# Gathering the experts' rows by token lists in place of scattering them: a state-space layer and a mixture of experts on one core

## The chip, the core and the metric

The kernel runs on one core of a Trainium2 chip. The metric is device time in microseconds (us) of one execution, the median of three runs. A second number is the span of a profiled execution, from its first instruction to its last.

## What is computed

Two batches of 1024 tokens of width 256 pass a state-space layer and then a mixture of experts, each behind a layer norm with a modulation computed from a small vector. Cut to what matters:

```python
h = _layernorm(x) * (1 + ca) + sa
x = x + ga * mamba(h)            # 512 channels x 16 states: h[t] = dA[t] * h[t-1] + dBu[t]; y = sum_s(h * C)
h = _layernorm(x) * (1 + cb) + sb
x = x + gb * ffn(h)              # 8 experts, top 2 of each token

gate_logits = einsum('bsd,de->bse', h, gate_kernel)
top_k_weights, top_k_indices = top_k(gate_logits, 2); weights = softmax(top_k_weights)
inter = silu(h @ w0[e]) * (h @ w1[e])
out = sum over the token's two experts of weight * (inter @ wo[e])
```

## The kernel before

The program is written out by hand for the five engines, each with its own instruction stream; semaphores order them. "Rows" of a tile are its 128 partitions. There are four stages.

**Stage A, projections.** A loop over the 2 batches. PE multiplies the normed tokens with the weights for x, dt, B and C (`project`, L449 to 453), always 128 channels x 1024 tokens into two PSUM banks. DVE copies each C product (`copy_C`, L978 to 983) into one of two slots of `C_st`, and SP stores the slot to `C_scratch` in DRAM twice (`C_to_dram`, L314 to 317), under two semaphores that `copy_C` waits for before it writes the slot again. B goes out in three bf16 parts (L329, 330). After the loop PE computes z (L512 to 516), 8 products into two pairs of banks, and ACT takes each through silu into `szT`, which lies over `C_st`; so ACT first waits until all copies of C have landed (L782 to 784). Stage A ends with a barrier of PE, DVE, ACT and POOL: each drains and raises `a_over`, and all wait for 4 (L517, L790, L1024, L1296; SP at L342).

**Stage B, scans.** 8 groups of 128 channels x 16 states, 128 steps in all. For a step PE spreads B over the partitions (`front`), DVE multiplies it with `du` (`drive`, L1033; for 4 of 16 states ACT copies it out and POOL multiplies, `share`, L1333), ACT computes the decay (L800), DVE scans 1024 tokens (L1045), POOL multiplies with C (`weigh`, L1310), and PE sums over states (`back`, L553). The C of a step comes from DRAM into one of four slots of `crep` (L356): 16 stored rows (8 heads, each there twice), each read for 8 partitions; a slot is asked for again when the product from it is done. Every second step SP also sends 261 KB of zeros to the rows' scratch (`zeros`, L337 to 339; `expert_in_scratch`, 17408 rows). A second barrier, `b_over`, ends the stage.

**Stage C, output projection and routing.** PE projects 16 tiles of 128 tokens (`outward_y`), DVE adds them to x and norms them, PE turns each tile (`turn_h2`, L593) and computes the gate's logits (L602), DVE picks two experts of each token (`pick`) and finds the place of each pair of token and expert in its expert's list (`place_of`, L1145 to 1158) from counts that PE makes (`ranks`, L605 to 617). This goes in quarters of 4 tiles, one quarter behind the other in DVE's fixed order (L1163 to 1197). POOL writes the 2048 tokens' rows, 261 numbers each, to the places, with one indirect DMA for each tile and each of the two choices: 32 (`send`, L1356). Small tables (L1199 to 1222) then give each of 39 slots of 128 rows its expert and its first row. A third barrier, `c_over`, ends the stage. SP then loads `wo` and waits until all 32 writes have landed (`sent`, L382) before it loads the first slot (L388).

**Stage D, experts.** For each of the 39 slots: SP loads 128 rows (L388) into one of two slots of `xg`, two slots ahead; PE turns them (L639), multiplies with w0 and w1 (L651), turns the product (L659), multiplies with wo (L667); ACT and DVE do the rest between; POOL adds the slot's results into the output with an indirect DMA (L1379), one after the other. In iteration i of the loop PE's order is: turn slot i+2, turn the product of i, hidden product of i+1, output product of i. DVE also takes each row's position, batch, expert and weights out of columns 256 to 260 (L1240 to 1245).

## Time and profile before

| | |
|---|---|
| median of 3 runs | 943.36 us (943.11 to 946.33) |
| profiled execution | 951.12 us, its span 949.3 us |
| granted TensorE clock, mean | 0.914 |
| busy share of the span | PE 79%, DVE 67%, POOL 53%, PEld 39%, ACT 34% |
| chain of waits, by engine | PE 43%, DVE 22%, POOL 10%, issue 10%, DMA 7%, ACT 6% |
| moved by DMA | 137.05 MB, mean 144 GB/s |

All times in this document are us on the profiled execution's own scale, where the first instruction starts at 0. Stage A runs to about 166, stage B from there to 603, stage C to 705, stage D to the end. The busy shares mix these four. The granted clock tells which share of 2.4 GHz TensorE got in a stretch: 1.00 is 2.4 GHz and 0.50 is 1.2 GHz.

### The profile page before, as it was taken

To read this page: it belongs to the slowest core of one execution; us is meant where nothing else is said; L and a number is where in the kernel's file an instruction comes from. 1 tells how busy PE (TensorE), PEld (TensorE's weight loads), DVE (VectorE), ACT (ScalarE), POOL (GpSimd) and SP (SyncE) were. 2 spreads that over 40 slices of the span, in tenths; PEclk is the share of its full clock that TensorE was granted. 3 is DMA by queue.
4 is the path that set the end of the run, shared out by engine and by line. 5 is a ranking of instruction groups with operands and counts; after the bars stand their busy time and mean duration, and the time that the engine had idled before them with its cause. 6 is when DMAs were issued, how large, how long until landed. Compare 5 with 4: busy or idle time off the path is not lost.

```text
span 949.3 us, 10338 instructions
## 1 busy us (share of the span) xinstructions
PE 749.2 (79%) x2240; PEld 368.4 (39%) x2241; DVE 639.7 (67%) x878; ACT 324.5 (34%) x360; POOL 502.0 (53%) x263
## 2 busy tenths in 40 slices
PE   5888969388878687787878787875329999999995
PEld 2433324132322232222323232564215666666663
DVE  4355662599999999899999999555504444444442
ACT  1564663445444444445444444001011111111110
POOL 1000000399999999999999999414622222222222
PEclk9898988599999998989999899986559999999998
DMA  9354540687877777777777688561361222222220
GB/s 260 96 136 146 131 142 0 174 219 200 220 201 213 185 221 192 200 182 217 209 191 213 185 219 221 183 241 68 113 221 35 42 44 44 44 43 43 43 38 0
DMA packets 75004, 137.05 MB, mean 144 GB/s; under 512 B 11426, under 2 KB 47586, under 8 KB 74852
## 3 DMA queue, kind: packets, MB, share of 16 engines
q1 hardware_dynamic: 64620, 127.97, 48.5%
q0 software_dynamic: 7152, 8.48, 5.3%
q10 hardware_dynamic: 3208, 0.34, 0.3%
q8 instruction: 8, 0.13, 0.1%
q14 instruction: 16, 0.13, 0.0%
HBM read 93.82 MB, written 39.66 MB: 141 GB/s over the span
## 4 chain that ended last, share of the span: by engine, by line
PE 43%; DVE 22%; POOL 10%; issue 10%; DMA 7%; ACT 6%; SPq 2%; ACTq 1%; POOLq 1%; DVEq 0%
DVE pool L1045 16%; PE PS L651 14%; PE PS L667 7%; PE PS L452 7%; PE PS L553 6%; ACT PS L800 4%; POOL pool L1310 4%; DMA C_scratch<-Y 4%; PE PS L584 3%; POOL spread L1333 3%; POOL expert_in_scratch L1360 2%; PE PS L659 2%; DVE pool L1033 2%; PE PS L535 1%; PE PS L639 1%
## 5 line engine op out<-in xcount | busy, mean ns | idle before, releaser
L1310 POOL TENSOR_TENSOR pool<-pool,hT 128x1024 f32<-128x1024 f32 x128 | 298.6, 2358 | 21.3 <-PE PS L553 17.4
L553 PE MATMUL PS<-pool,ident 128*128 128x512 f32 x512 | 261.1, 634 | 45.5 <-POOL pool L1310 45.3
L1045 DVE TENSOR_TENSOR_SCAN pool<-PS,pool 128x1024 f32<-128x1024 f32 x96 | 215.7, 2274 | 0.0
L800 ACT ACTIVATE PS<-pool,negA 128x1024 f32 (+1 forms) x128 | 143.1, 1118 | 195.9 <-DVE pool L1045 195.8
L1379 POOL DMA_INDIRECT out<-uT,ptab x39 | 60.6, 1554 | 184.3 <-DVE uT L1256 177.7
L553 PEld LDWEIGHTS PS<-pool,ident 128*128 128x128 f32 x512 | 96.0, 197 | 154.4 <-POOL pool L1310 74.8
L1033 DVE TENSOR_TENSOR pool<-PS,pool 128x1024 f32<-128x1024 f32 x96 | 117.6, 1225 | 40.9 <-PE PS L535 31.6
L651 PE MATMUL PS<-pool,uT 128*128 x312 | 142.6, 600 | 0.8 <-ACT uT L864 0.4
L535 PE MATMUL PS<-pool 96*128 96x512 bf16 x256 | 81.8, 403 | 54.7 <-DVE pool L1033 44.2
L1302 POOL TENSOR_TENSOR pool<-pool,uT 128x1024 f32<-128x1024 f32 (+1 forms) x8 | 18.9, 2359 | 143.0 <-ACTq L790 143.0
L1230 DVE TENSOR_TENSOR uT<-uT,PS 128x512 f32<-128x512 f32 x39 | 26.9, 689 | 92.8 <-PE PS L651 90.0
L1333 POOL TENSOR_TENSOR spread<-spread,pool 128x1024 f32<-128x1024 f32 x32 | 75.6, 2363 | 13.9 <-ACT spread L806 13.9
L651 PEld LDWEIGHTS PS<-pool,uT 128*128 128x128 f32 x312 | 57.0, 193 | 58.6 <-issue 58.6
L1045 DVE TENSOR_TENSOR_SCAN pool<-PS,spread 128x1024 f32<-128x1024 f32 x32 | 73.1, 2283 | 9.4 <-POOL spread L1333 9.4
L535 PEld LDWEIGHTS PS<-pool 96*128 96x128 bf16 x256 | 21.1, 101 | 149.0 <-DVE pool L1033 99.8
L667 PE MATMUL PS<-Y,uT 128*128 x312 | 73.8, 379 | 0.9 <-DVE uT L1235 0.9
L452 PE MATMUL PS<-hT,pool 128*128 x112 | 59.7, 686 | 12.2 <-DVE Y L983 12.2
L667 PEld LDWEIGHTS PS<-Y,uT 128*128 128x128 f32 x312 | 59.2, 190 | 25.3 <-issue 19.3
L864 ACT ACTIVATE uT<-PS 128x256 f32<-128x256 f32 x39 | 15.0, 385 | 144.1 <-PE PS L639 144.1
L870 ACT ACTIVATE uT<-PS 128x512 f32<-128x512 f32 x39 | 23.3, 598 | 74.6 <-PE PS L651 74.6
L1360 POOL DMA_INDIRECT expert_in_scratch<-pool,posu x32 | 31.7, 990 | 28.0 <-DVEq L1158 18.9
L806 ACT ACTIVATE spread<-PS 128x1024 f32<-128x1024 f32 x32 | 32.8, 1024 | 35.0 <-PE PS L535 35.0
(163 smaller groups left out, 699.9 us busy)
## 6 DMA issues: line engine op xcount, KB each, us to landing
hT<-C_scratch SPq DMA_DIRECT2D x128, 512.0 KB, 5.7
expert_in_scratch<-zrow SPq DMA_DIRECT2D x68, 261.0 KB, 5.8
C_scratch<-Y SPq DMA_DIRECT2D x16, 512.0 KB
pool<-in_w SPq DMA_DIRECT2D x16, 512.0 KB, 10.0
uT<-expert_in_scratch SPq DMA_DIRECT2D x39, 130.5 KB, 2.1
Y<-Y SPq DMA_DIRECT2D x32, 128.0 KB, 2.4
Y<-in_wo SPq DMA_DIRECT2D x8, 512.0 KB, 10.5
x_tok<-in_x SPq DMA_DIRECT2D x4, 512.0 KB, 8.9
```

What stands on the lines that cost most here:

```text
L452: m = pe.matmul(PS[:, bank + half, :], w(k), rhs(k, half), start=k == 0, stop=k == k_chunks - 1)
L535: m = pe.matmul(PS[:, 4 + half, :], sel[0:PARTS * 32, k, :], stk[0:PARTS * 32, r, HF * half:HF * half + HF], start=True, stop=True)
L553: m = pe.matmul(PS[:, 6 + half, :], ident[:, :], prod[:, k % PR, HF * half:HF * half + HF], start=False, stop=k == DS - 1)
L651: m = pe.matmul(PS[:, bank, :], xgT[:, r, k, :], w[:, bass.ds(e, 1), k, :].rearrange("p e n -> p (e n)"), start=k == 0, stop=k == KD - 1)
L667: m = pe.matmul(PS[:, 6 + r, 0:DM], intT[:, r, k, :], wo_sb[:, bass.ds(e, 1), k, :].rearrange("p e n -> p (e n)"), start=k == 0, stop=k == ...
L800: act.activation(pair(2 * (k % 2)).unsqueeze(1), delta[:, bass.ds(g2 * 2 + r, 1), :], ACT.Exp, scale=decay[:, bass.ds(g2 * (2 * DS) + n, 1 ...
L1033: dve.tensor_tensor(dbu[:, owned_to(k) % 2, :], pair(4), du[:, r, :], ALU.mult).then_inc(dbu_done, 1)
L1045: dve.tensor_tensor_scan(hst[:, k % HR, :], pair(2 * (k % 2)), driven, 0.0, ALU.mult, ALU.add).then_inc(scan_done, 1)
L1310: gp.tensor_tensor(prod[:, k % PR, :], hst[:, k % HR, :], crep[:, k % RC, :], ALU.mult).then_inc(prod_done, 1)
L1333: gp.tensor_tensor(spread[:, :], spread[:, :], du[:, r, :], ALU.mult).then_inc(shared_done, 1)
L1360: gp.indirect_dma_start(out=xs_dram, out_offset=bass.IndirectOffsetOnAxis(ap=posu[:, i, t:t + 1], axis=0), in_=h2row[:, t, :], in_offset=N ...
L1379: gp.indirect_dma_start(out=out, out_offset=bass.IndirectOffsetOnAxis(ap=ptab[:, slot:slot + 1], axis=0), in_=yo[:, slot % 2, :], in_offse ...
```

## The change

**C and B in DRAM.** C is stored once, by one DMA whose source and target are both 128 rows of 1024; the stored array has 8 rows for a step, and the load of a step reads each of them for 16 partitions. B goes out in four DMAs of 32 partitions x 3 parts.

**Barriers.** `a_over` and `b_over` are gone; each engine waits for the semaphores of the data that it uses. SP loads the first B parts after the first product of z, and the first C after the last. The decay rates (`negA`) are computed early in stage A. At the end of stage B PE runs the projection of tiles 0 to 2 between its last sums (before those of states 14 and 15).

**Rows by gather.** The zeros and the 32 writes are gone. Tokens' rows (260 numbers) go to DRAM in the tokens' own order, by 4 plain DMAs from SP. For each pair of token and expert its place p is split into p/128 and p mod 128; DVE makes a one-hot of each (16 operations for a quarter, one of each pair times the token's distance from the end), and PE multiplies the two, 8 products for a quarter, all added up in one PSUM bank: a table of tokens by place. One more product picks, for each slot, its row of that table. POOL then gathers each slot's 128 rows with an indirect DMA (`rows_of`, L1371), two slots ahead of the adds in its own order; `wo` is loaded in stage C.

```diff
-        C_dram = nc.dram_tensor("C_scratch", (2 * NB * DIN, L), F32, kind="Internal").ap()
-
-        C_twice = C_dram.rearrange("(h d s) n -> h d s n", d=2, s=DS)
-        C_rows = C_dram.rearrange("(h s) n -> h s n", s=DS)
+        C_dram = nc.dram_tensor("C_scratch", (NB * DIN, L), F32, kind="Internal").ap()
...
-                    for d, landed in enumerate((C_out[c % 2], C_again[c % 2])):
-                        sp.dma_start(C_twice[bass.ds(b * (DIN // DS) + c * HC, HC), d], C_st[:, c % 2, :]).then_inc(landed, 16)
+                    sp.dma_start(C_dram[bass.ds(b * DIN + c * P, P), :], C_st[:, c % 2, :]).then_inc(C_out[c % 2], 16)
...
-                for part in range(PARTS):
-                    sp.dma_start(B_dram[bass.ds(b * CH, CH), part], B_parts[:, part, :]).then_inc(B_out, 16)
+                for c in range(CH):
+                    sp.dma_start(B_dram[bass.ds(b * CH + c, 1)].rearrange("g a i n -> i (g a) n"),
+                                 B_parts[32 * c:32 * c + 32, :, :]).then_inc(B_out, 16)
...
-            def zeros(i):
-                sp.dma_start(xs_dram[bass.ds(i * (ZS * P), ZS * P), :].rearrange("(n p) c -> p n c", p=P),
-                             zrow[:, :].rearrange("p (n c) -> p n c", c=XW)).then_inc(xs_zeroed, 16)
...
-                                     C_rows[bass.ds((g2 * 2 + r) * 2 * HC, 2 * HC), k, :]
-                                     .unsqueeze(1).broadcast_to([2 * HC, DS // 2, L])).then_inc(crep_in[k % RC], 16)
-                        if k % 2 == 0:
-                            zeros((g2 * 2 + r) * 8 + k // 2)
+                                     C_dram.rearrange("(h s) n -> h s n", s=DS)[bass.ds((g2 * 2 + r) * HC, HC), k, :]
+                                     .unsqueeze(1).broadcast_to([HC, DS, L])).then_inc(crep_in[k % RC], 16)
...
+            sp.wait_ge(z_mm, 1)
             B_of(0, 0)
+            sp.wait_ge(z_mm, NB * CH)
...
-            sp.wait_ge(sent, 16 * 2 * NT)
-
-            def row_of(slot):
-                return sp.value_load(rtab[0:1, bass.ds(slot, 1)], min_val=0, max_val=XR - P)
-
-            def rows_in(first, r):
-                sp.dma_start(xg[:, r, :], xs_dram[bass.ds(first, P), :]).then_inc(xg_in[r], 16)
...
+            def h2_to_dram(q):
+                tiles = slice(TQ * q, TQ * q + TQ)
+                sp.wait_ge(weighted, q + 1)
+                sp.dma_start(h2_dram.rearrange("(t p) c -> p t c", p=P)[:, tiles, :], h2row[:, tiles, :]).then_inc(h2_out, 16)
...
-            pe.drain().then_inc(a_over, 1)
-
-
-            pe.wait_ge(sel_done, 1)
-            pe.wait_ge(a_over, 4)
+            pe.wait_ge(sel_done, HB)
+            pe.wait_ge(dt_free, 1 + NB * CH)
+            pe.wait_ge(C_copied, 1 + NB * CH)
...
+                        if last and r == 1 and k == DS - 2:
+                            outward_y(0)
+                            outward_y(1)
+                        elif last and r == 1 and k == DS - 1:
+                            outward_y(2)
...
+            def tokens_by_place(q):
+                pe.wait_ge(placed, q + 1)
+                for i in range(2):
+                    for j in range(TQ):
+                        m = pe.matmul(PS[:, 3, 0:P], by_place[i][:, j, :], by_row[:, i, j, :],
+                                      start=q == 0 and i == 0 and j == 0, stop=q == NQ - 1 and i == 1 and j == TQ - 1)
+                m.then_inc(place_mm, 1)
...
+            pe.wait_ge(turned_back, 2)
+            pe.matmul(PS[:, 6 + NQ % 2, 0:NS], token_by, slot_at, start=True, stop=True).then_inc(token_mm, 1)
...
-                step(dve.tensor_copy(posu[:, :, tiles], posf[:, q]))
+                step(dve.tensor_copy(pos_i, posf[:, q]))
+                settled()
+                step(dve.tensor_scalar(places[:, 0], pos_i, 7, None, ALU.arith_shift_right))
+                step(dve.tensor_scalar(places[:, 1], pos_i, P - 1, None, ALU.bitwise_and))
+                settled()
+                step(dve.tensor_copy(place_f, places))
+                settled()
+                if q:
+                    dve.wait_ge(place_mm, q)
+                else:
+                    dve.wait_ge(noted, 2)
+                for i in range(2):
+                    for j in range(TQ):
+                        step(dve.tensor_scalar(by_place[i][:, j, :], iota128, place_f[:, 0, i, j:j + 1],
+                                               from_end[:, TQ * q + j:TQ * q + j + 1], ALU.is_equal, ALU.mult))
+                        step(dve.tensor_scalar(by_row[:, i, j, :], iota128, place_f[:, 1, i, j:j + 1], None, ALU.is_equal))
...
+            dve.tensor_scalar(slot_at, slot_at, since[:, :], None, ALU.is_equal).then_inc(turned_back, 1)
+            dve.wait_ge(place_mm, NQ)
+            dve.tensor_copy(token_by, PS[:, 3, 0:P]).then_inc(turned_back, 1)
+            dve.wait_ge(token_mm, 1)
+            step(dve.tensor_scalar(ptab[:, :], PS[:, 6 + NQ % 2, 0:NS], -1.0, float(T), ALU.mult, ALU.add))
+            settled()
+            step(dve.tensor_scalar(gtab[:, :], ptab[:, :], float(T - 1), None, ALU.min))
...
-            def send(q):
-                gp.wait_ge(placed, q + 1)
-                for t in range(TQ * q, TQ * q + TQ):
-                    for i in range(2):
-                        gp.indirect_dma_start(out=xs_dram, out_offset=bass.IndirectOffsetOnAxis(ap=posu[:, i, t:t + 1], axis=0),
-                                              in_=h2row[:, t, :], in_offset=None).then_inc(sent, 16)
...
+            def rows_of(slot):
+                gp.indirect_dma_start(out=xg[:, slot % 2, :], out_offset=None, in_=h2_dram,
+                                      in_offset=bass.IndirectOffsetOnAxis(ap=gtab[:, slot:slot + 1], axis=0)).then_inc(xg_in[slot % 2], 16)
+
+            def refill(slot):
+                gp.wait_ge(xT_mm, slot - 1)
+                gp.wait_ge(meta_done, 3 * (slot - 1))
+                rows_of(slot)
+
...
+            gp.wait_ge(c_over, 3)
+            gp.wait_ge(h2_out, 16 * NQ)
+            rows_of(0)
+            rows_of(1)
+            gp.wait_ge(x2_out, 16 * NQ)
+            gp.sem_inc(yo_free, 2)
+            refill(2)
+            for slot in range(NS):
+                if slot + 3 < NS:
+                    refill(slot + 3)
+                leave(slot)
```

What moves, in the order of the engines' rows. On SP, the stores of stage A, for one batch; the name left of the arrow is the scratch in DRAM, and the sizes are the target's. Before:

```order
L330 DMA B_parts_scratch<-pool 4x32x1024
L330 ISA
L330 DMA B_parts_scratch<-pool 4x32x1024
L317 ISA [waits C_copied]
L317 DMA C_scratch<-Y 8x16x1024
L317 ISA
L317 DMA C_scratch<-Y 8x16x1024
```

and now:

```order
L331 DMA B_parts_scratch<-pool 32x3x1024
L331 ISA
L331 DMA B_parts_scratch<-pool 32x3x1024
L318 ISA [waits C_copied]
L318 DMA C_scratch<-Y 128x1024
```

One store for each C product, and outer sizes of 32 and 128 in place of 4 and 8.

On DVE, `place_of` in stage C, one quarter (`hT` holds the routing's small tables). Before:

```order
L1148 TENSOR_TENSOR hT<-PS,hT 128x32 [waits rank_mm]
L1152 TENSOR_TENSOR hT<-hT 128x64 [waits route_step]
L1154 TENSOR_REDUCE hT<-hT 128x8 [waits route_step]
L1156 CAST posu<-hT 128x2x4 [waits route_step]
L1096 SCALAR_TENSOR_TENSOR hT<-x_tok,mv,grow 128x256 [waits route_step,aggr2_done,h2_rows]
```

and now (six pairs like the two shown follow before L1090):

```order
L1150 TENSOR_REDUCE hT<-hT 128x8 [waits route_step]
L1152 CAST hT<-hT 128x8 [waits route_step]
L1154 TENSOR_SCALAR hT<-hT 128x8 [waits route_step]
L1155 TENSOR_SCALAR hT<-hT 128x8
L1157 CAST hT<-hT 128x16 [waits route_step]
L1165 TENSOR_SCALAR hT<-hT,from_end 128x128 [waits noted,route_step]
L1167 TENSOR_SCALAR spread<-hT 128x128
L1165 TENSOR_SCALAR hT<-hT,from_end 128x128
L1167 TENSOR_SCALAR spread<-hT 128x128
```

The 16 one-hots stand between the places and the norm of the next quarter.

On POOL, from the routing into stage D. Before:

```order
L1360 DMA expert_in_scratch<-pool,posu 17408x261 [waits placed]
L1360 DMA expert_in_scratch<-pool,posu 17408x261 x7
L1360 DMA expert_in_scratch<-pool,posu 17408x261 [waits placed]
L1360 DMA expert_in_scratch<-pool,posu 17408x261 x7
L1379 DMA out<-uT,ptab 2048x256 [waits x2_out,yo_done]
L1379 DMA out<-uT,ptab 2048x256 [waits yo_done,added] x38
```

and now:

```order
L1372 DMA uT<-expert_in_scratch,gtab 128x260 [waits h2_out,c_over]
L1372 DMA uT<-expert_in_scratch,gtab 128x260
L1372 DMA uT<-expert_in_scratch,gtab 128x260 [waits x2_out,meta_done,xT_mm]
L1372 DMA uT<-expert_in_scratch,gtab 128x260 [waits meta_done,xT_mm]
L1385 DMA out<-uT,ptab 2048x256 [waits yo_done]
L1372 DMA uT<-expert_in_scratch,gtab 128x260 [waits meta_done,xT_mm]
L1385 DMA out<-uT,ptab 2048x256 [waits yo_done,added]
L1372 DMA uT<-expert_in_scratch,gtab 128x260 [waits meta_done,xT_mm]
```

The gather of slot i+4 stands directly behind the add of slot i; before, the loads were on SP and stood behind no add.

## Rows read from the trace of the kernel before

**Rows 1.** costliest groups of the page: shapes, count, busy us, mean ns, idle before, releaser
```profile
L1310 POOL TENSOR_TENSOR pool<-pool,hT 128x1024 f32<-128x1024 f32 x128 | 298.6, 2358 | 21.3 <-PE PS L553 17.4
```

**Rows 2.** DMA issues of the page: count, KB each, median us from issue to landing
```profile
hT<-C_scratch SPq DMA_DIRECT2D x128, 512.0 KB, 5.7
expert_in_scratch<-zrow SPq DMA_DIRECT2D x68, 261.0 KB, 5.8
...
uT<-expert_in_scratch SPq DMA_DIRECT2D x39, 130.5 KB, 2.1
```

**Rows 3.** stretches: us, busy by engine, PEclk, share of 16 DMA engines, GB/s
```profile
119.00:122.00 3.00, 2.10 (x5) 0.68 (x4) 0.11 (x1) 2.97 (x4) 0.00 (x0) 1.00 0.51 209
250.00:300.00 50.00, 40.76 (x100) 15.10 (x100) 48.56 (x28) 22.92 (x22) 47.27 (x21) 0.97 0.77 206
650.00:683.00 33.00, 14.06 (x95) 10.60 (x95) 21.11 (x113) 3.47 (x11) 22.31 (x23) 0.50 0.23 82
```

**Rows 4.** the chain of waits: start us, us, what
```profile
56.63 16.20 DMA C_scratch<-Y
...
130.97 8.73 DMA C_scratch<-Y
```

**Rows 5.** DVE in time, stage A: start, us, instruction, idle before and releaser
```profile
72.86 1.22 DVE L983 COPY Y<-PS 128x1024 f32<-128x1024 f32 x1 [6.76 <-DMA C_scratch<-Y]
```

**Rows 6.** PE in time, stage A and its end
```profile
74.14 6.54 PE L452 MATMUL PS<-hT,pool 128*128 x8 [4.50 <-DVE Y L983]
82.24 7.13 PE L452 MATMUL PS<-hT,pool 128*128 x16 [1.56 <-DVE Y L983]
...
123.17 5.40 PE L452 MATMUL PS<-hT,pool 128*128 x8 [2.08 <-DVE Y L983]
...
142.49 23.67 PE L452 MATMUL PS<-hT,wz_sb 128*128 x48 [7.05 <-ACT Y L788]
```

**Rows 7.** PE in time, the first product of stage B
```profile
175.23 1.03 PE L535 MATMUL PS<-pool 96*128 96x512 bf16 x2 [9.08 <-DMA pool<-B_parts_scratch]
```

**Rows 8.** POOL in time, the first shared step of stage B
```profile
182.35 2.35 POOL L1333 TENSOR_TENSOR spread<-spread,pool 128x1024 f32<-128x1024 f32 x1 [12.40 <-ACT spread L806]
```

**Rows 9.** PE in time, end of stage B
```profile
601.26 1.98 PE L553 MATMUL PS<-pool,ident 128*128 128x512 f32 x4 [0.32 <-POOL pool L1310]
604.49 14.08 PE L584 MATMUL PS<-wout,uT 128*128 128x256 f32 x64 [1.24 <-ACTq L835]
```

**Rows 10.** DVE in time, eight 128x256 operations with two column operands
```profile
16.72 2.67 DVE L908 TENSOR_SCALAR Y<-x_tok,mv,rstd 128x256 f32<-128x256 f32 x8 [1.76 <-POOL rstd L1294]
```

**Rows 11.** PE in time, the routing, and its first work on experts
```profile
652.57 0.69 PE L593 MATMUL PS<-ident,pool 128*128 128x128 f32 x2 [4.85 <-DVE pool L1102]
653.74 1.02 PE L602 MATMUL PS<-gate_sb,hT 128*128 128x8 f32 x4 [0.47 <-ACT hT L844]
...
704.92 0.69 PE L639 MATMUL PS<-ident,uT 128*128 128x128 f32 x2 [29.48 <-DMA uT<-expert_in_scratch]
```

**Rows 12.** DVE in time, after the last table of the routing
```profile
683.07 0.43 DVE L1259 TENSOR_TENSOR grow<-grow 128x256 f32<-128x256 f32 x1
```

**Rows 13.** line 1360, scattered writes: duration ns min/median/max, and landing
```profile
L1360 POOL DMA_INDIRECT expert_in_scratch<-pool,posu x32: 957/961/1303, 651.3 to 696.0; - x32
...
DMA to landing us min/median/max: 2.4/2.8/7.1
```

**Rows 14.** line 1379, adds into the output: the same
```profile
L1379 POOL DMA_INDIRECT out<-uT,ptab x39: 1550/1551/1618, 721.8 to 940.3; - x39
...
DMA to landing us min/median/max: 2.7/3.9/4.5
```

**Rows 15.** PE in time, the first product of two successive slots
```profile
807.41 0.38 PE L639 MATMUL PS<-ident,uT 128*128 128x128 f32 x2
...
813.23 0.38 PE L639 MATMUL PS<-ident,uT 128*128 128x128 f32 x2
```

**Rows 16.** POOL in time, the same stretch
```profile
814.95 1.55 POOL L1379 DMA_INDIRECT out<-uT,ptab  x1 [4.27 <-DVE uT L1256]
```

More of the change, by code:

```diff
@@ L374, in _, with x2_to_out @@
                     sp.dma_start(dst[:, e], src[e].rearrange("(k p) n -> p k n", p=P)).then_inc(w01_in, 16)
-            for q in range(NQ):
+            sp.wait_ge(gated, CH * NB)
+            for e in range(NE):
+                sp.dma_start(wo_sb[:, e], wo[e].rearrange("(k p) n -> p k n", p=P)).then_inc(wo_in, 16)
+            def x2_to_out(q):
                 tiles = slice(TQ * q, TQ * q + TQ)
@@ L555, in back, with outward_y @@
                 m.then_inc(ysum_done, 1)
+            def outward_y(t):
+                b, at = t // NTB, t % NTB * P
+                if t == 0:
+                    pe.wait_ge(folded, 2)
+                    pe.wait_ge(gated, CH)
+                if t in (0, 2):
+                    pe.wait_ge(scan_done, 2 + NG * DS - (t == 0))
+                if t == NTB:
+                    pe.wait_ge(gated, CH * NB)
+                if t >= 3:
+                    pe.wait_ge(x2_step, t - 2)
+                for k in range(CH):
+                    m = pe.matmul(PS[:, t % 3, 0:DM], uT[:, b * CH + k, at:at + P], (wout0, wout_sb)[b][:, k, :],
+                                  start=k == 0, stop=k == CH - 1)
+                m.then_inc(o_mm, 1)
             def blocks_of(g2, last):
@@ L623, in _ @@
                     ranks(stage - 3)
+                    tokens_by_place(stage - 3)
                 for i in range(TQ):
@@ L719, in _, with decay_rates @@
             act.wait_ge(mod_step, 2)
+            def decay_rates():
+                act.wait_ge(acol_in, 16)
+                for n in range(NB):
+                    act.activation(negA[:, n, :], acol[:, :, :].rearrange("p c s -> p (c s)"), ACT.Exp).then_inc(col_done, 1)
             for b in range(NB):
+                if b:
+                    decay_rates()
                 for j in range(2):
@@ L1183, in _ @@
                         gathered(t)
+                if stage == 0:
+                    gate_y(CH + 3)
+                    route_tables()
                 if 0 <= stage - 3 < NQ - 2:
@@ L1207, in _ @@
             step(dve.tensor_tensor_scan(off, onef, cnt, 0.0, ALU.mult, ALU.add))
-            step(dve.tensor_scalar(fall, cnt, float(-P), float(T), ALU.mult, ALU.add))
+            step(dve.tensor_scalar(fall, cnt, float(-NT), None, ALU.add))
             settled()
@@ L1381, in _ @@
                                       compute_op=ALU.add).then_inc(added, 16)
+            for q in range(NQ):
+                rstd_of(q)
+            gp.wait_ge(c_over, 3)
[9 more added lines that the diff above has]
+                leave(slot)
             gp.wait_ge(added, 16 * NS)
```

205 lines of the change are left out of this document (81 added, 124 removed).

## The prediction

> **What bounds the kernel now.** I read the page's busy shares and slices, then the chain of waits, then each stage in time on the engines that wait there, then stretches and DMA rows. PE's 79% is a mean over stages with different limits. In stage A the chain runs through the C stores: one DMA of 16.20 and one of 8.73 us stand on it [rows 4], and DVE waits 6.76 us for a slot [rows 5]. Between A and B, PE runs z for 23.67 us [rows 6] and then waits 9.08 for B [rows 7]. In stage B a step takes (601.26 - 182.35) / 128 = 3.27 us [rows 8, 9]. DVE and POOL share this bound: of 50 us DVE is busy 48.56 and POOL 47.27, PE 40.76 [rows 3]; POOL's product alone is 298.6 us, 2.36 a step [rows 1]. The 16 DMA engines are busy 0.77 of that stretch [rows 3]. In stage C, DVE and PE alternate at a granted clock of 0.50 [rows 3], and behind the last table (683.07) [rows 12] PE waits until 704.92 for the written rows, 29.48 us of idle time [rows 11]. In stage D a slot takes 813.23 - 807.41 = 5.82 us [rows 15]; POOL's add waits 4.27 for its data in it [rows 16], so POOL has room.
>
> **The change part by part.** The sum is made against the profiled execution (951.12), 7.8 us above the median of the runs (943.36); I add it to the median.
>
> 1. *C stores, -15.* For the first batch's C copy DVE gets its slot 6.76 us late, at 72.86 [rows 5]; PE waits for that copy 4.50, and its next 8 matmuls take 6.54, where 16 take 7.13 at the full clock just behind, so 3.57 for 8 [rows 6]: 4.5 + 3.0 = 7.5 us. In the second batch the same place costs 2.08, and 5.40 - 3.57 = 1.83 [rows 6]: 3.9. Together 11.4, if a single store lands within the slot's turn. The stores move 209 GB/s at a share of 0.51 of the engines [rows 3], and half as many bytes go out. The last store holds z's ACT back, and through the PSUM banks PE, 7.05 us [rows 6]; 8.73 us of two DMAs [rows 4] become one of 4.4 (half) to 5.7 (the landing of 512 KB in stage B [rows 2]), so 3 to 4 more. Sum -15, bounds -16 and -11 (last store gives nothing).
> 2. *Barrier and B loads, -9.* z ends at 142.49 + 23.67 = 166.16 [rows 6], B is used at 175.23 [rows 7]. Loads requested behind z's first product are there long before. What comes behind, 182.35 - 175.23 = 7.1 us to the first shared product [rows 7, 8], stays. C is requested behind z's last product and is first needed at the end of those 7.1 us; a load takes 5.7 [rows 2]. If it is late by the rest, -7; if PE's work on B slips in between z's products, -10. I take -9.
> 3. *End of the scans, -2.* Eight tiles of the projection run behind the last sums, 604.49 + 14.08 = 618.57 [rows 9]. A tile is 1.76 us; three of them (5.3) go into waits for POOL's last products, of 2.36 each less 1.98 of sums [rows 1, 9], and most of what they save is met again by DVE's norms. Bounds -3 and 0.
> 4. *Stage B, 0.* The zeros were off the chain. Their cover isn't needed: each of the 128 steps keeps its instructions, and the C load has four slots, so some three steps (9.8 us) of time. This costs nothing as long as a 512 KB load uses the engines for under 3.27 us; see the first rival.
> 5. *One-hots on DVE, +14.* Eight 128x256 operations with two column operands take 2.67 us, 0.334 each [rows 10]. A 128x128 one is between half of it, 0.167, and all of it. I take 0.18, near half, since in such rows the elements carry the time. 16 x 0.18 + three more small operations at 0.2 = 3.5 us a quarter, four quarters 14. They stand in DVE's order ahead of the next quarter's norm, for which PE waits (4.85 before a turn) [rows 11], so all of it is on the path. Bounds 12.8 and 23.7 (0.334 each).
> 6. *Token products on PE, +7.* 8 products a quarter, two matmuls each (f32), at 0.345 (0.69 / 2) or 0.255 (1.02 / 4) [rows 11]: 5.5 or 4.1 us; taken 4.5, at the low clock as now. For the first quarters PE has room while DVE norms, but DVE's wait on the counts stands behind these products in PE's order: 1.5 us each for two of them, and about 4.2 before the last counts. Bounds 0 (all in PE's idle time) and +10.
> 7. *Tail of the tables, +2.5.* Behind the last one-hots come the last 8 products, a copy, one product and two small operations; 4.5 for the products is in point 6, the rest is 2 to 3.
> 8. *Scattered writes gone, -18.* From the last table to PE's first work on experts 704.92 - 683.07 = 21.85 us [rows 11, 12]. Those writes were issued between 651.3 and 696.0, 0.96 each [rows 13]. In their place: 0.9 for the gather's issue and a handoff, and 2.8 to land (median of the writes [rows 13]): -18.1. With points 5 to 7 routing and its tail come out at +5.4. If POOL's norms or the rows' store (82 GB/s is moved there, share 0.23 [rows 3]) come late, the gather comes later; I count that in the bounds.
> 9. *Expert loop, +13.* Here a wait is added: POOL's gather of slot i+4 stands behind the add of slot i. The add starts 7.54 us behind PE's first work of slot i's iteration (814.95 - 807.41) and takes 1.55 [rows 15, 16]. The gather is then asked for at 9.4, and takes L to land. PE needs it two slots later, so 2T >= 9.4 + L. The plain load took 2.1 [rows 2], a scattered write 0.96 + 2.8 less the overlap, an add 3.9 [rows 13, 14]. With L = 2.9, T = 6.15 against 5.82: 38 x 0.33 = +13. Bounds: L = 2.2 gives 5.82, +1; L = 3.9 gives 6.65, +31. I take 2.9 as a gather reads and doesn't add, as the write does.
>
> The Trainium skill bears on this ("DMA: Bandwidth & Descriptors", Anatomy of one DMA, SWDGE path): a GpSimd DMA takes some 2.0 us plus its bytes at 436 GB/s. By that a gather of 133 KB lands in 2.3, an estimate, T is 5.85 and the loss of point 9 is 1 us. The rows of writes and adds lie above it.
>
> Sum: -15 - 9 - 2 + 0 + 14 + 7 + 2.5 - 18 + 13 = -7.5, rounded with the halves -8: **935 us**. Its own range, bounds combined without taking all at their ends: 918 to 955.
>
> **The rivals.**
>
> *The C loads become the bound of the scans (slower).* The load now reads 8 rows, each for 16 partitions. Stores of C with an outer size of 8 kept only 0.51 of the engines busy [rows 3], as if eight of the sixteen worked, while loads with 16 outer rows reach 0.77. If the outer size sets how many work, the loads get eight. In stage B 206 GB/s at 0.77 of 16 engines is 16.7 GB/s each [rows 3]; eight move 134 GB/s, a load needs 3.92 us, and a step grows from 3.27 to 3.92: 128 x 0.65 = +83, at 1018. But in the C stores an engine moved 209 / (0.51 x 16) = 25.6 GB/s [rows 3]; at that rate eight carry 205, a load needs 2.56 and stays hidden. It decides at 524,288 B / 3.27 us = 160 GB/s for the eight. For it: the same bytes are read by sixteen partitions, and the loads' own rate is the low one. Against: the zeros, which share the engines now, are gone, and eight that don't compete may each be faster. Time 955 to 1018. The Trainium skill has the rule ("DMA: Bandwidth & Descriptors", Why a DMA increments its semaphore by 16 and not by 1): a copy is spread over the largest number of engines, up to 16, that divides the outermost dimension of both sides. By that rule the new load gets eight; the trace agrees for the stores of before, and no row of it shows a load with eight rows.
>
> *Gathers are late and the routing is long.* L = 3.9 (+18 over the forecast), or one-hots at 0.334 (+10): about 953. For it: an add takes 3.9 [rows 14]. Against: an add writes and sums, a gather only reads.
>
> *Gathers on time.* Slots stay at 5.85, 12 less: 924. For it: the plain load's 2.1 [rows 2].
>
> *The stores don't get faster.* If a single C store lands as late as the pair (8.73 [rows 4]), stage A keeps its waits and point 1 is lost: 950, the same as no change.
>
> **How the numbers follow.** Forecast 0.38; C loads as the bound 0.28; late 0.12; on time 0.14; stores no faster 0.08. Within 0.5% (all that a measurement of this kernel can tell from no change) is 938.6 to 948.1. Faster: 0.25 of the forecast and the 0.14 on time, 0.40. Same: 0.09 of the forecast (above 938.6, as its bounds of +14 and +31 reach there), 0.02 of late, 0.02 of the loads' case where it is only just missed, 0.05 of the stores': 0.18. Slower: the rest, 0.42, most of it from the C loads. The likeliest case alone gives 918 to 955. The range goes up to 1000, which leaves out the upper end of the C loads' case and little below 918.
>
> **What would show it.** In stage A, DVE's C copies wait for no DMA and z's matmuls end near 151. The first shared product of stage B starts near 158. Stage B: 3.27 us a step means point 4 holds; a longer one with PE, DVE or POOL released by the DMA of C is the first rival, and the landing of C loads (5.7 now [rows 2]) then rises above three steps. A share of 16 engines near 0.5 with the loads hidden shows eight engines that suffice. In stage C: the one-hots' mean (0.18), the token products (4.5 a quarter), first work on experts some 5 us later behind the projection's start than now. In stage D: a slot of 6.15, PE released by the gather, and the gather's landing of 2.9; 5.82 would show the rival on time. What makes the prediction wrong most is a C load above 3.27 us; next a gather's landing, of which each us is 19.

## The result, and the profile after

The changed kernel takes 972.23 us (median of 4 runs, 969.86 to 981.74), the kernel before 943.57 (943.11 to 946.33): a ratio of 1.0316, 95% interval 1.0245 to 1.0388. It is slower; 935 was forecast. The time lies in the range that was given. The first rival, the C loads, is what happened in part, and the expert loop lost more than was counted.

The two profiled executions differ by 971.0 - 949.3 = 21.7 us of span, 7 less than the medians, since the profiled one of before lay 7.8 above its own median. By place (a mark is the start of a row unless said):

| mark | before | after | moved by |
|---|---|---|---|
| end of z | 166.16 | 140.29 | -25.9 |
| first shared product | 182.35 | 147.35 | -35.0 |
| end of POOL's last product with C | 601.21 | 593.15 | -8.1 |
| first product on experts | 704.92 | 697.33 | -7.6 |
| span | 949.3 | 971.0 | +21.7 |

So stage A and the barrier gave 35.0 us, the scans took back 26.9, the routing 0.5, and the expert loop 29.3.

Stage A in time, PE (start, us, instruction, idle before and releaser). The wait of 4.50 before 8 matmuls of 6.54 and the one of 7.05 inside z [rows 6] are gone, and B is there when z ends [rows 7]:

```profile
66.84 3.60 PE L438 MATMUL PS<-hT,pool 128*128 x8
71.84 7.13 PE L438 MATMUL PS<-hT,pool 128*128 x16 [1.41 <-DVE Y L980]
...
112.29 28.00 PE L438 MATMUL PS<-hT,wz_sb 128*128 x64
140.12 0.60 PE L519 MATMUL PS<-pool 96*128 96x512 bf16 x2
```

The first and the last product of the scans, POOL. The last one waits for the DMA of C:

```profile
147.35 2.34 POOL L1351 TENSOR_TENSOR spread<-spread,pool 128x1024 f32<-128x1024 f32 x1 [28.08 <-ACT spread L810]
...
590.59 2.56 POOL L1328 TENSOR_TENSOR pool<-pool,hT 128x1024 f32<-128x1024 f32 x1 [0.74 <-DMA hT<-C_scratch]
```

The chain of waits in the scans (start, us, what). Before, no DMA stood on it there:

```profile
283.35 14.84 DMA hT<-C_scratch
...
300.81 13.61 DMA hT<-C_scratch
...
317.06 13.60 DMA hT<-C_scratch
```

A load is asked for 13.6 to 14.8 us before it lands, four steps at once in the queue, and then POOL runs one product at a time.

Two stretches of the scans (columns as in [rows 3]):

```profile
230.00:365.00 135.00, 96.59 (x214) 35.08 (x215) 107.59 (x61) 50.56 (x47) 109.21 (x48) 0.91 0.51 135
365.00:440.00 75.00, 57.46 (x142) 21.46 (x141) 70.78 (x41) 35.33 (x33) 72.05 (x32) 0.98 0.49 161
```

The share of the 16 engines is one half in both, 0.77 before [rows 3], as if eight of them worked all the time. By the Trainium skill ("DMA: Bandwidth & Descriptors", Why a DMA increments its semaphore by 16 and not by 1) 8 outer rows give eight engines, and here the trace agrees. What those eight move differs: 135 GB/s (16.5 each) in the first stretch, 161 (20.5 each) in the second. POOL does 48 operations in 135 us (2.81 us for each) and 32 in 75 (2.34). The bound that the prediction gave, 160 GB/s, parts the two.

The 161 is what the scans ask for and not what the eight can do. Short windows show that:

```profile
480.00:490.00 10.00, 8.46 (x22) 2.95 (x20) 9.79 (x7) 5.16 (x6) 9.07 (x5) 1.00 0.51 129
500.00:505.00 5.00, 3.72 (x10) 1.26 (x9) 2.60 (x2) 1.55 (x2) 4.43 (x2) 1.00 0.51 192
355.00:360.00 5.00, 4.50 (x9) 1.39 (x8) 3.29 (x2) 0.98 (x1) 5.00 (x3) 0.67 0.51 203
```

At the same share of 0.51 the same kind of load runs at 129 / (0.51 x 16) = 15.8 GB/s for each engine in the first of them, at 23.5 in the second and at 24.9 in the third. These are the two prices of the first rival, 134 and 205, in one execution.

The routing. One-hots by DVE, one pair after the other, and the token products behind the first quarter:

```profile
639.26 0.35 DVE L1165 TENSOR_SCALAR hT<-hT,from_end 128x128 f32<-128x128 f32 x1
639.52 0.28 DVE L1167 TENSOR_SCALAR spread<-hT 128x128 f32<-128x128 f32 x1
639.72 0.34 DVE L1165 TENSOR_SCALAR hT<-hT,from_end 128x128 f32<-128x128 f32 x1
```

```profile
643.09 2.08 PE L613 MATMUL PS<-spread,hT 128*128 128x128 f32 x8 [7.09 <-DVEq L1169]
644.96 1.92 PE L613 MATMUL PS<-spread,by_place 128*128 128x128 f32 x8
...
697.33 0.69 PE L639 MATMUL PS<-ident,uT 128*128 128x128 f32 x2 [4.04 <-DMA uT<-expert_in_scratch,gtab]
```

A pair takes 639.72 - 639.26 = 0.46 us (the rows overlap), so 16 operations some 3.6; PE waits 4.04 where it waited 29.48 [rows 11].

The expert loop, two slots, PE and then POOL. Every second turn waits for a gather:

```profile
732.77 0.43 PE L639 MATMUL PS<-ident,uT 128*128 128x128 f32 x2 [0.54 <-DMA uT<-expert_in_scratch,gtab]
733.04 0.60 PE L659 MATMUL PS<-ident,uT 128*128 128x128 f32 x4
734.00 3.69 PE L651 MATMUL PS<-pool,uT 128*128 x8 [0.36 <-ACT uT L865]
737.54 1.89 PE L667 MATMUL PS<-Y,uT 128*128 x8
739.26 0.38 PE L639 MATMUL PS<-ident,uT 128*128 128x128 f32 x2
...
745.82 0.43 PE L639 MATMUL PS<-ident,uT 128*128 128x128 f32 x2 [0.51 <-DMA uT<-expert_in_scratch,gtab]
```

```profile
741.03 1.59 POOL L1385 DMA_INDIRECT out<-uT,ptab  x1 [4.31 <-DVE wsel L1260]
742.92 0.99 POOL L1372 DMA_INDIRECT uT<-expert_in_scratch,gtab  x1 [0.30 <-issue]
```

Two slots take 745.82 - 732.77 = 13.05 us, 6.53 each against 5.82 [rows 15]. The add starts 8.26 behind the turn, 1.59 and 0.30 follow, and 2.90 behind the start of the gather PE runs again: 13.05.

DMA issues of the page (KB each, median us to landing):

```profile
C_scratch<-Y SPq DMA_DIRECT2D x8, 512.0 KB, 2.6
...
B_parts_scratch<-pool SPq DMA_DIRECT2D x8, 192.0 KB, 3.0
...
uT<-expert_in_scratch,gtab POOLq DMA_INDIRECT x39, 2.8
```

### The profile page after: what moved, and what is told of

Same layout as the page of the kernel before. It is cut to its first block, busy times and chain, and to the rows that moved or that the text cites. A ratio compares the mean times of both kernels' runs of the same rounds, so it can differ in the third digit from the quotient of the medians.

```text
span 971.0 us, 9913 instructions
## 1 busy us (share of the span) xinstructions
PE 771.7 (79%) x2306; PEld 378.9 (39%) x2307; DVE 660.5 (68%) x918; ACT 322.6 (33%) x359; POOL 511.9 (53%) x270
## 4 chain that ended last, share of the span: by engine, by line
PE 36%; DMA 20%; DVE 15%; POOL 14%; issue 9%; ACT 4%; ACTq 0%; DVEq 0%; POOLq 0%; SPq 0%
DMA hT<-C_scratch 13%; PE PS L651 9%; PE PS L438 8%; DVE pool L1037 8%; POOL pool L1328 8%; PE PS L537 6%; DMA uT<-expert_in_scratch,gtab 6%; PE PS L667 3%; PE PS L553 3%; POOL spread L1351 3%; POOL out L1385 3%; ACT PS L804 2%; PE PS L659 2%; PE PS L519 1%; PE PS L639 1%
## 5 line engine op out<-in xcount | busy, mean ns | idle before, releaser
L537 PE MATMUL PS<-pool,ident 128*128 128x512 f32 x512 | 269.8, 652 | 73.9 <-POOL pool L1328 73.7
L651 PE MATMUL PS<-pool,uT 128*128 x312 | 145.2, 608 | 9.1 <-ACT uT L865 7.9
L1037 DVE TENSOR_TENSOR_SCAN pool<-PS,spread 128x1024 f32<-128x1024 f32 x32 | 73.1, 2286 | 25.6 <-POOL spread L1351 25.4
L1372 POOL DMA_INDIRECT uT<-expert_in_scratch,gtab x39 | 38.8, 994 | 69.0 <-DVEq L1243 55.9
L438 PE MATMUL PS<-hT,pool 128*128 x112 | 51.0, 601 | 5.5 <-DVE Y L980 5.5
L810 ACT ACTIVATE spread<-PS 128x1024 f32<-128x1024 f32 x32 | 32.8, 1024 | 35.6 <-PE PS L519 35.6
```

Of the source, the lines that this page charges most:

```text
L438: m = pe.matmul(PS[:, bank + half, :], w(k), rhs(k, half), start=k == 0, stop=k == k_chunks - 1)
L537: m = pe.matmul(PS[:, 6 + half, :], ident[:, :], prod[:, k % PR, HF * half:HF * half + HF], start=False, stop=k == DS - 1)
L651: m = pe.matmul(PS[:, bank, :], xgT[:, r, k, :], w[:, bass.ds(e, 1), k, :].rearrange("p e n -> p (e n)"), start=k == 0, stop=k == KD - 1)
L1037: dve.tensor_tensor_scan(hst[:, k % HR, :], pair(2 * (k % 2)), driven, 0.0, ALU.mult, ALU.add).then_inc(scan_done, 1)
L1372: gp.indirect_dma_start(out=xg[:, slot % 2, :], out_offset=None, in_=h2_dram, in_offset=bass.IndirectOffsetOnAxis(ap=gtab[:, slot:slot + 1 ...
```

## The experiments

The theory after the result: two losses in two stages, C loads on eight engines and gathers queued behind adds. "Scans" below is the time from the start of the first shared product to the end of POOL's last product with C, in the profiled execution: 418.9 us before, 445.8 after. The kernel before took medians of 946.3 to 948.8 beside these runs; each ratio is against its own.

**Gather ahead of the add.**

```diff
             refill(2)
+            refill(3)
             for slot in range(NS):
-                if slot + 3 < NS:
-                    refill(slot + 3)
+                if slot + 4 < NS:
+                    refill(slot + 4)
                 leave(slot)
```

> The changed kernel with one edit: POOL asks for the gather of slot i+4 ahead of the add of slot i, not behind it. If the expert loop grew because each gather is queued behind an add (it is asked for 8.3 us behind the start of the slot's iteration, of 13.1 for two slots), a slot falls from 6.55 back to 5.8 or 5.9 us, PE no longer waits for the gather, and the kernel gets 25 us faster, some 947 us. Rival: the gather itself is too slow, or adds and gathers slow each other in the DMA engines; then a slot stays above 6.3 and the time within 10 us of 972. Stages A to C must not move.

Measured: 946.8 us, single runs 923.2, 946.6, 947.0 and 954.4. The expert loop falls to 952.6 - 706.8 = 245.8 us (244.4 before), and PE no longer waits for a gather:

```profile
821.71 0.38 PE L639 MATMUL PS<-ident,uT 128*128 128x128 f32 x2
...
827.52 0.38 PE L639 MATMUL PS<-ident,uT 128*128 128x128 f32 x2
...
833.34 0.38 PE L639 MATMUL PS<-ident,uT 128*128 128x128 f32 x2
```

5.82 us a slot: the order on POOL was the whole loss of the loop. A gather still lands in 2.8, so it wasn't the gather's own speed. The median moved by 25.4, but the spread of the runs is new. In the profiled run, the slowest of the four, the scans took 452.3 us, with a long slow stretch:

```profile
360.00:495.00 135.00, 95.88 (x212) 34.31 (x212) 105.97 (x60) 51.02 (x47) 105.46 (x46) 0.90 0.52 131
```

That the run of 923.2 had no such stretch is likely, but it has no trace. The slow stretches don't lie where they lay in the changed kernel (some 240 to 350), though the same rows of C are read at the same place in the order; so which rows are read doesn't decide it alone.

**C copied in DRAM, loads over 16 rows.** The store keeps its 128 rows and goes to a scratch of its own; two DMAs for each product then fill the layout of before, in which a load finds its 16 rows.

```diff
+    for d in range(2):
+        sp.dma_start(C_dram.rearrange("(h d s) n -> s d h n", d=2, s=DS)[:, d, rows],
+                     C_once.rearrange("(h s) n -> s h n", s=DS)[:, rows]).then_inc(C_twice, 16)
...
-    C_dram.rearrange("(h s) n -> h s n", s=DS)[bass.ds((g2 * 2 + r) * HC, HC), k, :]
-    .unsqueeze(1).broadcast_to([HC, DS, L])
+    C_dram.rearrange("(h s) n -> h s n", s=DS)[bass.ds((g2 * 2 + r) * 2 * HC, 2 * HC), k, :]
+    .unsqueeze(1).broadcast_to([2 * HC, DS // 2, L])
```

> The changed kernel with C stored once from the SBUF as it is, then copied twice in DRAM (outer size 16 on both sides), so that a load again reads 16 rows, each for 8 partitions. If the scans are slower because a load with an outer size of 8 runs on 8 of the 16 engines, the landing falls, POOL no longer waits for C, and a step falls from 3.44 on average to 3.27 us: 128 steps give 21 us, some 951 us. Stage A stays as in the changed kernel, since nothing on PE's path waits for the copies. Rival: the loads aren't the cause, but the removed barrier or the other order at the start of the scans; then stage B stays at 440 us.

Measured: 949.9 us over ten runs (ratio 1.0027, 1.0000 to 1.0054, without two of them at 959), 22 less than the changed kernel; scans 419.2 us. In the same stretch as above:

```profile
230.00:365.00 135.00, 105.35 (x253) 38.94 (x252) 126.60 (x72) 60.69 (x57) 129.81 (x57) 0.95 0.61 162
```

57 operations on POOL where there were 48. Each engine moves no more than in the slow stretch (162 / 9.8 = 16.6 GB/s), but sixteen can serve. The rate of an engine didn't have to change; their number did. One thing isn't parted here or in any other run: a load over sixteen engines always reads 16 stored rows and a load over eight reads 8. No run reads 8 rows with sixteen engines.

**Both edits.**

> Both edits. The two losses lie in stages that follow one another, so they add: 972 less 21 less 25 gives 926 us, faster than the kernel before by 1.8%. If the gain is under 40 us, one of the two hid behind the other.

Measured: 924.6 us, ratio 0.9756 (0.9715 to 0.9797). The losses add, 47.6 us in all. Scans 421.8 us, expert loop 245.3. Against the version before it (949.9) this is the cleaner price of the order on POOL, as neither has slow stretches: 25 us.

**The kernel before with 8-row loads.**

> The kernel before, in which only the load of C is changed: it reads the 8 rows of the first copy, each for 16 partitions. The zeros (262 KB every second step) stay. If eight engines carry the loads and the zeros share them, the loads lose more than in the changed kernel: a step of 3.6 us or more, the kernel slower by 40 us or more (985). Rival: the source rows cost nothing of themselves and it was the order of the changed kernel: 943.

Measured: 950.4 us, ratio 1.0037 (1.0006 to 1.0068); scans 425.0 us. I expected 40 us or more and found 4, and no long stretch in which POOL waits for C:

```profile
230.00:365.00 135.00, 106.09 (x263) 39.56 (x261) 129.09 (x73) 62.59 (x58) 128.19 (x56) 0.97 0.59 206
```

Eight engines alone are not enough to lose the 27 us: something else in the change belongs to it.

**Rows 4352 bytes apart.**

```diff
-        C_dram = nc.dram_tensor("C_scratch", (NB * DIN, L), F32, kind="Internal").ap()
+        C_dram = nc.dram_tensor("C_scratch", (NB * DIN, L + 64), F32, kind="Internal").ap()[:, 0:L]
```

> The changed kernel with the gather first, and with the stored rows of C 4352 bytes apart in DRAM in place of 4096, so that the 8 rows of a load are no longer 65536 bytes apart. Loads stay on eight engines. If a load is slow (4.4 us in some stretches, 2.6 in others) because its rows fall on the same part of the memory, all loads take 2.6 us, are hidden, and the kernel takes some 922 us, as with 16 rows. Rival: the distance between rows has nothing to do with it; then the times spread over 923 to 954 us as with the gather first alone.

Measured: 931.3 us (930.7 to 934.9), scans 433.9 us. Neither of the two expectations: steadier than the gather first alone, but not 922, and one long stretch stays slow. All four runs lie inside the 923 to 954 of the gather first alone, so that the distance helped is likely and not shown.

```profile
230.00:365.00 135.00, 105.59 (x254) 39.16 (x254) 126.58 (x72) 61.12 (x57) 129.70 (x57) 0.95 0.48 160
500.00:560.00 60.00, 39.79 (x100) 14.26 (x98) 50.11 (x29) 24.08 (x22) 47.54 (x21) 1.00 0.51 135
```

**Two loads in flight, and one.** SP waits for the landing of two loads before (n = k - 2 in the group's count), or of one before (k - 1).

```diff
+                        n = r * DS + k - 2
+                        if n >= 0:
+                            sp.wait_ge(crep_in[n % RC], g2 * (2 * DS // RC * 16) + (n // RC + 1) * 16)
```

> The changed kernel with the gather first; SP asks for the C of a step only when the load of two steps before has landed (its loop over groups is written out for that). If loads are slow because up to four of them are queued at once, the slow stretches vanish and the time is 925 us or less. Rival: a load is slow whatever is queued behind it; then the wait only takes away room and the time is at or above 947 us.

Measured with two in flight: 919.5, 932.7, 943.6 and 944.4 us; scans 437.1 us in the profiled one. Slow stretches are still there:

```profile
246.00:290.00 44.00, 32.10 (x75) 11.88 (x75) 36.89 (x22) 17.71 (x17) 36.36 (x17) 0.94 0.52 134
```

> A look at the load alone: SP asks for the C of a step only when the load before has landed, so that each load starts with the queue empty. If loads are slow only back to back, the engines move as much as in the fast stretches of the changed kernel while they are busy (22 GB/s each or more, by the windows), even though each step now takes the load's whole time from issue to landing, some 4.5 us, and the kernel some 1080 us. Rival: the rate falls to 16 GB/s in some stretches here too; then it isn't the queue.

Measured with one in flight, one run: 1263.5 us, against my 1080, as a step now takes almost 6 us. Busy engines move 91 / (0.29 x 16) = 19.6 GB/s each here, 18.1 in the next row, neither 22 nor 16:

```profile
200.00:300.00 100.00, 65.77 (x108) 21.95 (x107) 54.86 (x31) 24.27 (x23) 51.41 (x22) 0.70 0.29 91
300.00:400.00 100.00, 64.53 (x105) 21.41 (x103) 51.05 (x29) 26.23 (x25) 52.64 (x23) 0.69 0.30 87
```

With two in flight the slow stretches stay, so a queue of four isn't what makes them. The run with one in flight decides nothing more: its rate is neither of the two.

**C stored twice again.** The two stores of before (outer size 8), in the kernel with the gather first.

> The changed kernel with the gather first and with C stored twice as in the kernel before (outer size 8) and loaded over 16 rows. Against the version that copies in DRAM (924.6 us) this prices the stores: if the single store was worth what stage A gained, DVE waits again for C slots and z's end comes 15 to 20 us later, 940 to 945 us. The barrier's 9 us stay saved. Rival: the pair of stores costs little once the B stores are faster: 928 us.

Measured: 924.6 us, ratio 0.9754 (0.9710 to 0.9798), scans 417.7. Neither time that I gave was met, the rival's 928 came nearest: z ends only 9.9 us later than in the changed kernel, and 9.2 of it lie inside z:

```profile
113.06 7.03 PE L442 MATMUL PS<-hT,wz_sb 128*128 x16
127.64 22.59 PE L442 MATMUL PS<-hT,wz_sb 128*128 x48 [7.55 <-ACT Y L797]
```

z starts at 113.06, as in the changed kernel (112.29), although C is stored twice.

**The kernel before with C stored once**, loaded over 8 rows; the rest as before.

> The kernel before, with C stored once by a DMA of 128 rows and loaded over 8 rows (65536 bytes apart); barriers, B stores, zeros and scattered writes stay. Stage A: z ends some 18 to 26 us earlier, but B still comes 9 us behind z. Stage B: if the locked slow loads need the queue to run empty of zeros, a step stays near the 3.32 us that the 8-row load alone gave (425 us in all), and the kernel takes some 930 us; if they come from the rows' distance (131072 bytes there, 65536 here), stage B takes 440 us or more and the kernel 945 or more.

Measured: 939.4 us, ratio 0.9882 (0.9827 to 0.9938); scans 424.5, a step of 3.32. Stage A and the end of the barrier:

```profile
117.52 7.03 PE L450 MATMUL PS<-hT,wz_sb 128*128 x16
126.93 20.87 PE L450 MATMUL PS<-hT,wz_sb 128*128 x48 [2.38 <-ACT Y L785]
156.86 1.03 PE L533 MATMUL PS<-pool 96*128 96x512 bf16 x2 [9.06 <-DMA pool<-B_parts_scratch]
```

Against the same kernel with two stores and 8-row loads, z starts 123.16 - 117.52 = 5.6 us and ends 160.29 - 147.80 = 12.5 us earlier. The rows lie as in the changed kernel, and still no stretch is slow. What both eight-row kernels without the loss have is the zeros, beside the barriers and the old order of SP.

**The zeros back.** A DMA of 256 KB behind every second load, in the kernel with the gather first.

```diff
+                        if k % 2 == 0:
+                            sp.dma_start(old_dram[bass.ds(((g2 * 2 + r) * 8 + k // 2) * (2 * P), 2 * P), :].rearrange("(n p) c -> p n c", p=P),
+                                         by_place1[:, :, :].rearrange("p t n -> p (t n)").rearrange("p (n c) -> p n c", c=256)).then_inc(old_out, 16)
```

> The changed kernel with the gather first, and with a DMA of 256 KB from the SBUF to DRAM behind every second load of C, where the zeros stood (packets of 1024 bytes; the routing waits for them at its start). Loads stay on eight engines. If a load gets slow when it follows another without a break, and the removed zeros were what kept the loads apart, the long stretches of slow loads vanish: stage B 422 to 427 us, and all runs near 925 us. Rival: the zeros only add traffic; then stage B takes 440 us or more in some runs, and the times spread up to 954 us or lie above it.

Measured: 928.5 us (920.6 to 930.5), ratio 0.9787 (0.9733 to 0.9840); scans 426.1. With 64 x 262144 bytes, 16.8 MB, more to move, the scans are 26 us shorter than in the profiled run without, which was the slowest of its four. All four runs here are at or under 930.5 us, where three of the four without were at 946.6 or above:

```profile
230.00:365.00 135.00, 105.65 (x253) 39.70 (x254) 126.38 (x72) 61.46 (x57) 129.72 (x57) 0.95 0.56 201
```

The two versions ran on different chips (the kernel before took 946.3 us on the one and 947.4 on the other). But on the chip of the gather first alone the eight-row kernel with zeros had scans of 425.0 against 452.3, and on a third chip the one with C stored once 424.5 against the 437.1 of two in flight. The edit also adds an array in DRAM, which could shift where C lies; the next version has the same array.

**4 KB in place of the 256.**

> As the version with the zeros back, but the DMA behind every second load moves 4 KB in all (128 pieces of 32 bytes), not 256 KB. If a break between two loads in the queue is what keeps them fast, this is enough: all runs at 920 to 930 us. Rival: it is the time that the zeros' bytes take on the engines that keeps the loads apart; then slow stretches come back and the times spread up to 954 us as with the gather first alone.

Measured: 931.7 us (927.2 to 938.3), scans 436.8, with slow stretches again: 129 GB/s at a share of 0.49 between 160 and 200 us. So the array in DRAM isn't the cure. The scans lie between those with 256 KB and those with nothing between the loads. Whether a short break helps at all can't be told from four runs; what 256 KB do, 4 KB don't.

**The 8 rows of a state side by side.**

```diff
-    sp.dma_start(C_dram[bass.ds(b * DIN + c * P, P), :], C_st[:, c % 2, :])
+    sp.dma_start(C_dram.rearrange("(g s h) n -> g h s n", h=HC, s=DS)[b * CH + c], C_st[:, c % 2, :])
```

> The gather first, and C stored so that the 8 rows of a state lie side by side in DRAM (32 KB in one piece; the store's outer size is 8). Loads on eight engines, outer size 8. If the slow loads come from reading rows that lie far apart, no load takes over 3 us and all runs are at 920 to 926 us. Rival: where the rows lie has nothing to do with it, the conflict is among the eight engines or where they write: stretches with 4.2 us a load and times up to 954 us.

Measured: 980.8 us (969.3 to 986.7), ratio 1.0384 (1.0328 to 1.0440), scans 462.4. My expectation was the wrong way round: close together is no cure, and all four runs lie above the 954 that the rival allowed. Some 9 us of it aren't the loads', as the store on eight engines lets z end at 149.85 in place of 140.98. In the one traced run, the fastest of the four, the loads are no slower than in the traced run of the gather first alone, the slowest of its four. A long stretch of both, gather first and then this one:

```profile
230.00:560.00 330.00, 249.27 (x576) 91.08 (x576) 287.30 (x162) 138.59 (x127) 288.39 (x125) 0.93 0.51 147
230.00:560.00 330.00, 244.90 (x568) 89.61 (x566) 285.34 (x161) 135.37 (x126) 289.86 (x125) 0.93 0.51 150
```

So a worse layout is what the times suggest, and what no trace shows.

**Half of the one-hots on POOL.** Built on the version with two stores.

> The version with the gather first and C stored twice (924.6 us), with 8 of the 16 one-hots of a quarter moved from DVE to POOL, which has nothing to do there. If all of the one-hots lie on the path, DVE's 8 x 0.2 = 1.6 us a quarter go, but PE then waits for POOL's eight if these take longer than DVE's eight: between 0 and 6 us faster. Rival: the two engines slow each other, and the time is above 925 us.

Measured: 934.3 us, ratio 0.9851 (0.9818 to 0.9885), 10 slower than its base and above the rival's 925. One such operation takes POOL 602 ns:

```profile
L1405 POOL TENSOR_SCALAR spread<-hT x32: 601/602/843, 626.4 to 678.8; 128x128 f32<-128x128 f32 x32
```

Eight take 4.7 to 5.3 us where DVE did all sixteen in 3.6, and PE's idle time before the token products grows from 7.09 to 8.81 us in the first quarter, by 5.6 over the four. From the last product with C to the first work on experts it is 107.8 us against 103.5 in the base: the path goes through the one-hots, and that is 4.3 of the 11.1 between the two profiled executions. The rest stands where nothing was changed: 2.2 up to the first shared product, 3.1 in the scans, 1.5 in the expert loop.

**The second copy made in DRAM from the first.** One store from the SBUF with outer size 8, one DRAM copy with outer size 16.

> The gather first, and C stored once from the SBUF (outer size 8) straight into the first copy, and the second copy made in DRAM (outer size 16). Loads over 16 rows. The single store on eight engines should cost stage A at most 2 us against the 128-row one, and there is half as much to copy: z ends at 142 us or before, stage B takes 418 to 422 us, and the time is 918 to 923 us, the best of all. Rival: the store on eight engines makes DVE wait for its slot: 925 us or more.

Measured: 924.0 us (921.0 to 928.3), ratio 0.9758 (0.9716 to 0.9799); z ends at 146.2, scans 421.4. The store on eight engines costs z a wait of 3.62, and the end of z is 5.9 us later than in the changed kernel where I allowed 2. The version isn't better than the two others with 16-row loads: all three take 924 to 925 us, 2.4% less than the kernel before and 48 less than the change as it came.

## Why the prediction was wrong

The step that failed is point 4, the scans at 0. It held that the load is hidden "as long as a 512 KB load uses the engines for under 3.27 us", and took that case for the likelier one. The rival had the mechanism, its two prices (134 and 205 GB/s) and the bound (160); both rates occur in one execution (129 to 135, and 192 to 203), so the loss was 26.9 us and not the +83 of its upper end. The undo (16-row loads) gives back 22 us. One sentence in it was wrong outright: that the missing zeros speak against the rival. With the zeros there, eight engines nearly suffice (scans 424.5 to 426.1, against 418.9 before and 417.7 to 421.8 with 16-row loads); without them they often don't. Why the zeros help stays open.

Point by point, with what the runs showed:

*Point 1, C stores, -15.* -25.9 in the profiled pair; mis-sized. The B stores (three DMAs of outer size 4, now four of 32) were costed at nothing, but the C stores stand behind them on SP. No run changes the B stores alone; what points to them is that with the new B stores and C still stored twice z starts at 113.1, against 123.2 in the 8-row-load run of before and 128.4 in the profiled run of before. The single C store alone gave 12.5, near the 15 of the forecast. And the wait of 7.05 inside z was counted at half and went whole. Some 6 us of the 25.9 are the profiled run's own: the same stage A code ended z at 160.29 in another run, which is most of the 7.8 that it lay above the median.

*Point 2, barrier, -9.* Measured 25.9 to 35.0: -9.1. Right, and the kernel before with C stored once, which keeps the barrier, still shows the wait of 9.06.

*Points 3 and 5 to 8, end of the scans and routing, -2 and +5.4.* Forecast together +3.4, measured 104.2 - 103.7 = +0.5 from the last product with C to the first work on experts. The one-hots took 3.6 us a quarter where 16 x 0.18 = 2.9 were counted, the token products 3.8 where 4.5 were. The lower bound of point 5 is also mis-added: with 0.167 for each its own terms give 13.1 and not 12.8. The sum came out near, and that is partly luck: the terms miss in both directions and weren't measured one by one. The one test of it, half of the one-hots on POOL, shows that they are on the path.

*Point 9, expert loop, +13.* Mechanism right, size off: +29.3. A gather landed in 2.8 (2.9 assumed; 2.3, by which the prediction worked out a loss of 1 us, is too low). The term that was mis-sized is the add's place. I read 7.54 us from a slot in which nothing was late. When PE starts again from a late gather, ACT's copy stands uncovered before the hidden product (0.36 idle). That product starts 734.00 - 732.77 = 1.23 behind the turn, and in the slot of before 808.07 - 807.41 = 0.66. Its matmuls take 3.69 for 3.60 too, and the add comes 8.26 behind the turn.

```profile
808.07 3.60 PE L651 MATMUL PS<-pool,uT 128*128 x8
```

That gives 6.53 a slot, and 38 x 0.71 = 27; the 2 us that are left of the 29.3 weren't traced. A small slip beside it: with L = 2.2 the formula gives 5.80, under the slot of 5.82, so the lower bound is 0 and not +1.

The forecast's sum was -8, the medians moved by +28.7. Of the 37 between them the scans are 27 and the expert loop 16; the routing (3 less than forecast) and stage A (11 less, of which some 6 or 7 only against the profiled run) take the rest back. The chances were too low on the C loads: 0.28, for what a row already showed in part: 16.7 GB/s for an engine in a stretch of loads and zeros, which is nearly what an engine moved in the slow stretches.

## What to carry to other kernels

Count the engines that a DMA uses before halving its bytes: eight engines with half of the source rows were worse here than sixteen with all of them. On an engine that issues DMAs, put what others wait for ahead of what nobody waits for; turning two lines round gave 25 us here. And price a loop-carried wait from the moment at which it releases the chain, not from a slot in which nothing was late.

## What the runs showed of the hardware that was not expected

A DMA of C over eight engines moves at two speeds in one execution. In stretches of tens of microseconds it is 129 to 135 GB/s, some 16 for each engine; elsewhere the same loads reach 192 to 203, some 24 or 25 each, at the same share of the engines. Some 160 is what the scans ask for on average. With two loads in flight in place of four the slow stretches stay. The distance of the eight rows may matter: side by side the kernel took 969 to 987 us (9 us of that lie in stage A), 65536 bytes apart 923 to 954, and 69632 apart 931 to 935. Four runs of each, and loads at 150, 147 and 157 GB/s in the one traced run of each (230 to 560 us), don't settle it. And other traffic between the loads, which should cost them time, makes them faster: with 256 KB behind every second load the four runs took 921 to 931 us. Two engines that come to the same part of the memory at once could give this, but no run shows it; that stays open. Loads over 16 rows show none of it, with scans of 417.7 to 421.8 us in five traces.
